# A hyperedge product of a four-layer graph network as two float32r passes, with its low part made on VectorE

## What is computed

```python
H = (adj != 0).astype(x.dtype)           # [N,C,C] indicator
w = adj.reshape(N, -1)[:, :C]            # first row of adj
Dn = jnp.einsum('nce,ne->nc', H, w)
Dn = jnp.where(Dn > 0, 1.0 / Dn, 0.0)
Be = H.sum(axis=1)
Be = jnp.where(Be > 0, 1.0 / Be, 0.0)
m = Be[:, :, None] * jnp.einsum('nce,nch->neh', H, xw)
out = Dn[:, :, None] * jnp.einsum('nce,neh->nch', H, m)
```

## Time and profile before

| | before |
|---|---|
| median of 3 runs | 1825.22 us (1825.14 to 1826.91) |
| the profiled execution: its time, its span | 1824.28 us, 1822.6 us |
| granted TensorE clock | 0.998 |
| busy: PE, DVE, ACT, POOL | 1771.0, 1416.4, 1443.2, 1442.6 us |
| one pass of the loop, from one e_cnt to that six passes on (767.32 to 1101.27 us) | 55.66 us |

### The profile page before, as it was taken

The page is one execution under the profiler, slowest core; times in us unless marked ns, Lnnn a source line. Parts: engine busy times, 40 slices in busy tenths (PEclk is TensorE's granted clock), DMA queues, the critical chain, the costliest instruction groups (busy, mean ns, idle before and its releaser), DMA issues.

```text
span 1822.6 us, 52146 instructions
## 1 busy us (share of the span) xinstructions
PE 1771.0 (97%) x15358; PEld 1569.1 (86%) x15358; DVE 1416.4 (78%) x3910; ACT 1443.2 (79%) x4463; POOL 1442.6 (79%) x2857
## 2 busy tenths in 40 slices
PE   7999999999999999999999999999999999999997
PEld 6888888888888888888888888888888888888886
DVE  6878778777778787787777787877877777878776
ACT  4888778887788887788877888877888777888776
POOL 4787778887788877788877888777888778887776
PEclk9999999999999999999999999999999999999999
DMA  4011101111001111011110011110111100111000
GB/s 129 22 42 41 36 13 32 40 40 40 18 28 35 40 40 37 12 32 40 40 40 20 26 35 40 40 37 12 32 40 40 40 20 26 35 40 40 29 9 22
DMA packets 93590, 62.94 MB, mean 35 GB/s; under 512 B 8430, under 2 KB 92924, under 8 KB 93564
## 3 DMA queue, kind: packets, MB, share of 16 engines
q1 hardware_dynamic: 92748, 61.58, 11.3%
q10 hardware_dynamic: 816, 1.05, 0.2%
HBM read 45.82 MB, written 16.78 MB: 34 GB/s over the span
## 4 chain that ended last, share of the span: by engine, by line
PE 62%; POOL 13%; issue 9%; DVE 8%; ACT 5%; ACTq 1%; SPq 1%; DMA 0%; POOLq 0%; DVEq 0%
PE ps L512 32%; PE ps L585 6%; PE ps L593 4%; PE ps L606 3%; POOL hT L928 3%; PE ps L617 3%; PE ps L528 3%; PE ps L576 3%; POOL ln_rs L882 3%; PE ps L496 3%; DVE z L1111 2%; ACT z L781 2%; PE ps L523 2%; POOL c L966 2%; POOL hb L934 2%
## 5 line engine op out<-in xcount | busy, mean ns | idle before, releaser
L781 ACT ACTIVATE z<-z,z_max 128x128 f32<-128x128 f32 x1024 | 401.0, 403 | 53.2 <-DVE z_max L1122 50.0
L882 POOL TENSOR_TENSOR ln_rs<-ln_ve,minus_half 128x1 f32<-128x1 f32 x640 | 352.6, 551 | 50.2
L902 POOL TENSOR_TENSOR z<-z,z_rcp 128x1024 f32<-128x1024 f32 x128 | 242.9, 1897 | 26.6 <-DVE z_rcp L1129 26.6
L885 POOL TENSOR_SCALAR ln_nm<-ln_mv,ln_rs 128x1 f32<-128x1 f32 x640 | 169.3, 264 | 109.8 <-POOL ln_rs L882 109.8
L880 POOL TENSOR_TENSOR ln_ve<-ln_mv,eps_col 128x1 f32<-128x1 f32 x640 | 121.8, 190 | 160.0 <-DVE ln_mv L1035 157.7
L1111 DVE SCALAR_TENSOR_TENSOR z<-ps,a_hold 128x512 f32<-128x512 f32 x256 | 171.1, 679 | 52.0 <-PE ps L576 48.7
L512 PE MATMUL ps<-w2T,mnT 128*128 128x256 f32 x1536 | 208.1, 287 | 0.0
L512 PE MATMUL ps<-w1T,txT 128*128 128x512 f32 x768 | 203.4, 400 | 0.9 <-DVE txT L1045 0.9
L781 ACT ACTIVATION_READ_ACCUMULATOR z<-z,z_max 128x1 f32 x1024 | 204.4, 200 | 0.0
L512 PEld LDWEIGHTS ps<-w2T,mnT 128*128 128x128 f32 x1536 | 188.8, 188 | 5.6 <-DVE mnT L1045 0.2
L1122 DVE TENSOR_REDUCE z_max<-z 128x4 f32<-128x512 f32 x256 | 169.5, 673 | 0.1
(11 more groups left out here) (154 smaller groups left out, 4864.4 us busy)
## 6 DMA issues: line engine op xcount, KB each, us to landing
x_in<-in_x_dram SPq DMA_DIRECT2D x128, 128.0 KB, 2.2
a_hold<-in_adj_dram SPq DMA_DIRECT2D x128, 128.0 KB, 2.2
out_dram<-y_out SPq DMA_DIRECT2D x128, 128.0 KB, 1.7
a_in<-in_adj_dram SPq DMA_DIRECT2D x128, 64.0 KB, 1.9
h<-in_L_gnn_W_dram SPq DMA_DIRECT2D x2, 512.0 KB, 5.7
x<-in_L_gnn_Wqk_dram ACTq DMA_DIRECT2D x1, 512.0 KB, 4.0
y_out<-in_L_gnn_W_dram ACTq DMA_DIRECT2D x1, 256.0 KB, 4.6
y_out<-in_L_gnn_Wv_dram ACTq DMA_DIRECT2D x1, 256.0 KB, 4.9
```

The source lines that it names most:

```text
L781: m = act.activation(z[:, g % 2, h, :], z[:, g % 2, h, :], ACT.Exp, bias=z_max[:, g % 2, h:h + 1], accum_out=z_sum[:, g % 2, h:h + 1])
L882: pool.tensor_tensor(rs[n][:, g:g + 1], ve[n][:, g:g + 1], minus_half[:, :], ALU.pow).then_inc(root_made[n], 1)
L885: pool.tensor_scalar(nm[n][:, g:g + 1], mv[n][:, g, 0:1], rs[n][:, g:g + 1], -1.0, ALU.mult, ALU.mult).then_inc(shift_made[n], 1)
L902: pool.tensor_tensor(zg, zg, z_rcp[:, g % 2, :].unsqueeze(2).to_broadcast([P, HEADS, P]), ALU.mult)\
```

## The change

The product `mp` becomes two float32r passes that accumulate in PSUM. The indicator hT is exactly 0 or 1 and is now stored as float32r; hb gets a high and a low part. POOL makes the high part from a rounded reciprocal `r_hi`. A new DVE step `hbl` stands right behind `ecnt` in both order texts and makes three things: the low part of the weight column, `r_lo` = e_rcp - r_hi, and the low part of hb, hT times r_lo. DVE's `ecnt` also makes r_hi. PE waits for `hb_made` before the high pass and for `hb_lo_made` before the low one. The other order texts are as they were.

```diff
-        ln4_aggr.1 ecnt.0+ mn_lo.2 z1.0+ mn_lo.3 zmax1.0+ y.2 z0.0+ ln4_stats.2 zmax0.0+ ln4_aggr.2 y.3
+        ln4_aggr.1 ecnt.0+ hbl.0+ mn_lo.2 z1.0+ mn_lo.3 zmax1.0+ y.2 z0.0+ ln4_stats.2 zmax0.0+ ln4_aggr.2 y.3
...
-        hT, hb, mp = sb("hT", G, P + 1), sb("hb", G, P + 2), sb("mp", G, P + 2)
+        hT = ctx.enter_context(nc.sbuf_tensor("hT", [P, G, P + 1], F32R))
+        hb, mp = parts("hb", G, P + 2), sb("mp", G, P + 2)
+        r_hi, r_lo = ctx.enter_context(nc.sbuf_tensor("r_hi", [P, G], F32R)), sb("r_lo", G)
...
             def mp_(a, g, o):
-                room(1, not need(hb_made, a))
-                return pe.matmul(o[:, 0:P + 2], hT[:, g, 0:P], hb[:, g, :], start=True, stop=True)
+                need(hb_made, a)
+                for part in (HI, LO):
+                    room(2 - part)
+                    if part == LO:
+                        need(hb_lo_made, a)
+                    m = pe.matmul(o[:, 0:P + 2], hT[:, g, 0:P], hb[:, part, g, :], start=(part == HI), stop=(part == LO))
+                return m
...
             def hb_(q, g):
                 pool.wait_ge(hT_made, q + 1)
-                pool.wait_ge(ercp_made, q + 1)
+                pool.wait_ge(rhi_made, q + 1)
                 after(pool, made["mp"], q * G)
-                pool.tensor_tensor(hb[:, :, 0:P], hT[:, :, 0:P], e_rcp[:, :].unsqueeze(2).to_broadcast([P, G, P]), ALU.mult)\
+                pool.tensor_tensor(hb[:, HI, :, 0:P], hT[:, :, 0:P].bitcast(F32),
+                                   r_hi[:, :].bitcast(F32).unsqueeze(2).to_broadcast([P, G, P]), ALU.mult)\
                     .then_inc(hb_made, 1)
...
-                dve.tensor_reduce(e_cnt[:, :], hT[:, :, :], AX.X, ALU.add).then_inc(cnt_made, 1)
-                dve.wait_ge(cnt_made, q + 1)
-                dve.reciprocal(e_rcp[:, :], e_cnt[:, :]).then_inc(ercp_made, 1)
+                dve.tensor_reduce(e_cnt[:, :], hT[:, :, :].bitcast(F32), AX.X, ALU.add).then_inc(edge_step, 1)
+                dve.wait_ge(edge_step, q * 4 + 1)
+                dve.reciprocal(e_rcp[:, :], e_cnt[:, :]).then_inc(edge_step, 1)
+                dve.wait_ge(edge_step, q * 4 + 2)
+                dve.tensor_copy(r_hi[:, :], e_rcp[:, :]).then_inc(rhi_made, 1)
+
+            def hbl(q, g, o):
+                after(dve, made["mp"], q * G)
+                dve.wait_ge(col_made, q + 1)
+                dve.tensor_tensor(hb[:, LO, :, P:P + 1], aT[:, :, 0:1], hb[:, HI, :, P:P + 1].bitcast(F32), ALU.subtract)\
+                    .then_inc(edge_step, 1)
+                dve.wait_ge(rhi_made, q + 1)
+                dve.tensor_tensor(r_lo[:, :], e_rcp[:, :], r_hi[:, :].bitcast(F32), ALU.subtract).then_inc(edge_step, 1)
+                dve.wait_ge(edge_step, q * 4 + 4)
+                dve.tensor_tensor(hb[:, LO, :, 0:P], hT[:, :, 0:P].bitcast(F32),
+                                  r_lo[:, :].unsqueeze(2).to_broadcast([P, G, P]), ALU.mult).then_inc(hb_lo_made, 1)
```

More of the change, by code:

```diff
@@ L110 @@
         turnlo.11+ ln1_stats.2+ ln1_aggr.2+ v1.3+ ln1_stats.3+ ln1_aggr.3+ x2t_lo.0+ turnlo.12+ turnlo.13+
-        turnlo.14+ x2t_lo.1+ x2t_lo.2+ x2t_lo.3+ turnlo.15+ turnlo.16+ c2lo.0+ lo_wo.0+ turnlo.17+ ecnt.0+
+        turnlo.14+ x2t_lo.1+ x2t_lo.2+ x2t_lo.3+ turnlo.15+ turnlo.16+ c2lo.0+ lo_wo.0+ turnlo.17+ ecnt.0+ hbl.0+
         turnlo.18+ turnlo.19+ scale.0+ scale.1+ z1.0+ zmax1.0+ z0.0+ scale.2+ zmax0.0+ scale.3+ z0.1+ z1.1+
@@ L156 @@
 HI, LO = 0, 1
-PASSES = {"at": 1, "ax": 2, "x1t": 2, "amx": 1, "wt": 1, "pb": 1, "x2t": 2, "mp": 1, "sc0": 4, "sc1": 4, "pt": 8, "cx": 8,
+PASSES = {"at": 1, "ax": 2, "x1t": 2, "amx": 1, "wt": 1, "pb": 1, "x2t": 2, "mp": 2, "sc0": 4, "sc1": 4, "pt": 8, "cx": 8,
           "tx": 2, "mn": 4, "y": 12, "turn": 1, "gram": 1, "c2": 1, "bw": 1}
@@ L285, in build @@
             "xb_made", "wm_made", "p_bias_made", "p_exp_made", "p_rcp_made"))
-        hT_made, col_made, cnt_made, ercp_made, hb_made = (sem(n) for n in (
-            "hT_made", "col_made", "cnt_made", "ercp_made", "hb_made"))
+        hT_made, col_made, edge_step, rhi_made, hb_made, hb_lo_made = (sem(n) for n in (
+            "hT_made", "col_made", "edge_step", "rhi_made", "hb_made", "hb_lo_made"))
         dsum_made, dmax_made, dpos_made, drcp_made, dhalf_made, dinv_made, dcnt_made, c3_half, c3_made = (sem(n) for n in (
@@ L659, in weights @@
                     need(read["turn"], a, last_turn["w1"])
-            counted_by_group = {read[s].name for s in per_group} | {s.name for s in (amT_made, wm_made, hb_made, col_made)}
+            counted_by_group = {read[s].name for s in per_group} | {s.name for s in (amT_made, wm_made, hb_made, hb_lo_made, col_made)}
             stages = {"at": at, "ax": ax, "h0": h0, "x1t": x1t, "amx": amx_, "xg": xg, "wt": wt, "pb": pb, "v1": v1,
@@ L754, in aT_free @@
                 after(act, amT_made, q)
-                after(act, hT_made, q)
-                after(act, col_made, q)
+                after(act, hb_lo_made, q)
             def mp_free(q, g):
@@ L775, in hbc @@
                 after(act, made["mp"], q * G)
-                act.copy(hb[:, :, P:P + 1], aT[:, :, 0:1]).then_inc(col_made, 1)
+                act.copy(hb[:, HI, :, P:P + 1], aT[:, :, 0:1]).then_inc(col_made, 1)
             def attn(q, g, half):
@@ L926, in hT_ @@
                 after(pool, made["mp"], q * G)
-                after(pool, cnt_made, q)
+                after(pool, edge_step, q * 4)
                 pool.tensor_scalar(hT[:, :, 0:P], aT[:, :, :], 0.0, 0.0, ALU.is_equal, ALU.is_equal).then_inc(hT_made, 1)
@@ L1183, in split @@
                 return run
-            stages = {"asum": asum, "h0": h0, "xg": xg, "wmax": wmax, "wnorm": wnorm, "pcol": pcol, "v1": v1, "ecnt": ecnt,
+            stages = {"asum": asum, "h0": h0, "xg": xg, "wmax": wmax, "wnorm": wnorm, "pcol": pcol, "v1": v1, "ecnt": ecnt, "hbl": hbl,
                       "drcp": drcp, "z0": z_(0), "z1": z_(1), "zmax0": zmax(0), "zmax1": zmax(1), "wo": wo, "h1": h1_, "y": y,
@@ L1217, in _ @@
             dve.memset(eps4_col[:, :], EPS / 4)
-            dve.memset(hT[:, :, P:P + 1], TINY)
+            dve.memset(hT[:, :, P:P + 1].bitcast(F32), TINY)
             dve.memset(p_row[:, :], 0.0)
-            dve.memset(hb[:, :, P + 1:P + 2], 1.0)
+            dve.memset(hb[:, HI, :, P + 1:P + 2].bitcast(F32), 1.0)
+            dve.memset(hb[:, LO, :, P + 1:P + 2].bitcast(F32), 0.0)
             walk(FIRST, -1)
```

## The result

| | before | after |
|---|---|---|
| median | 1825.14 us (1823.25 to 1826.91, 5 runs) | 1834.51 us (1833.5 to 1838.71, 5 runs) |
| profiled execution, span | 1822.6 us | 1832.7 us |
| one loop pass, e_cnt to e_cnt | 55.66 us | 55.98 us (771.20 to 827.18) |
| ratio after/before | | 1.0057, 95% interval 1.0042 to 1.0071 |

The change makes the kernel 9.4 us slower. The forecast was 1835.9 us, and the loop pass grew by 0.32 us where 0.33 was forecast. Part of that closeness is luck: two errors on the way, each as large as the forecast itself, cancel. ScalarE's exp0.0 came 0.32 us later than forecast, and 0.33 us were given back where the forecast had nothing.

A forecast was written before the change was run, and what follows sets the result against it. PE, 97% busy, was taken as nearly the bound, with a chain through other engines in each pass. 31 x 0.33 = 10.2 us plus 0.5 gave 10.7, from 1824.28 to 1835.0, median 1835.9 us; 8-in-10 range 1828 to 1858.

The forecast's parts named there:

- Where the delay starts: On PE, y.2 starts 0.06 us after DVE's mn_lo.2 ends, so TensorE was said to have no slack there.
- DVE's delay of 0.97 us: Four DVE instructions behind the reciprocal, the product priced 0.69 us, move mn_lo.2 0.97 us later, bounds 0.6 and 1.2.
- POOL's part is free: r_hi is ready 0.2 us after the reciprocal's end at 656.90; POOL takes up hb only at 657.85.
- What PE gives back: Lost PE time absorbs delay: 0.19 us in y.2 and y.3, 0.32 at the third mp product, 0.39 before v2.1.
- The narrow pass: A float32r pass of 130 columns takes 0.11 us, decided by weight loads, so 0.22 per product, as long as before.
- cheap rival: A narrow pass takes only 0.062 us; exp1.0 and three copies then set exp0.0, +0.24 per pass, 1833.1 us; chance 0.13.
- dear case: A narrow pass takes 0.22 us, 0.44 per product; exp0.0 comes 1.00 later per pass, 1856.7 us; chance 0.20.
- ACT decides, +0.33 per pass: The third mp product's copy makes ACT's exp0.0 0.33 us late; the dense work behind it gives nothing back.
- taken up elsewhere: Small DVE steps cost half and ACT's stretch to v2.2 hides a gap: under 0.1 us left, 1828 us; chance 0.07.
- The first filling: The pipeline's first filling has one more such delay, between 0 and 0.97 us, taken as 0.5 us.
- Faster: TensorE's own work decides, y.2 doesn't wait for mn_lo.2, each of 128 products saves 0.10 us: 1812.4 us; chance 0.05.

The follow-up runs named there:

- e2: Changed kernel with hb's low part zero from the start, step hbl gone, both float32r passes kept, four waits per aT copy as before: 1826.93 us, ratio 1.0013 to before.
- e4: Changed kernel with hT made by DVE ahead of e_cnt instead of by POOL: 1804.27 us, ratio 0.9891 to the kernel before.
- e1: Changed kernel with all DVE steps kept but the product one plain f32 product again: 1837.43 us, ratio 1.0070 to the kernel before.
- e8: Changed kernel with each float32r pass of the product streaming 240 instead of 130 columns: 1834.54 us, ratio 1.0034 to the kernel before.
- e9: Changed kernel whose low pass loads 64 of 128 stationary columns and doesn't add to the high pass: 1835.99 us, ratio 1.0060 to the kernel before.
- e3: Changed kernel with only the high float32r pass, step hbl gone, four waits per aT copy as before: 1827.52 us, ratio 1.0014 to the kernel before.
- e11: Kernel before with the waits hT_made and col_made ahead of each aT copy replaced by one, hb_made: 1820.18 us, ratio 0.9976 to before.
- e12: Kernel before with hT on DVE and the two waits ahead of each aT copy replaced by one: 1798.77 us, ratio 0.9856 to before.
- e5: Kernel before with hT made by DVE ahead of e_cnt, still four waits ahead of each aT copy: 1806.38 us, ratio 0.9881 to before.
- e10: Changed kernel with the waits hT_made and col_made put back ahead of each aT copy on ACT: 1846.8 us, ratio 1.0119 to the kernel before.
- e7: Changed kernel with step hbl moved behind zmax1.0 instead of ahead of mn_lo.2: 1881.13 us, ratio 1.0278 to the kernel before.

## Why the prediction was right, and where it was not

**Where the delay starts.** Right. The prediction saw that y.2 starts 0.06 us after mn_lo.2 ends and called it slackless; after the change PE waits there 31 times, and the waits vanish with the steps (e2) or when they move into DVE's idle time (e4). e1 and e2 show that in the place where the steps stand nothing else of the change costs.

**DVE's delay of 0.97 us.** Wrong, 1.42. The small steps were sized right (0.16 to 0.17 against 0.18, gaps included). The failed step is the price of the 128x512 product, "priced as its neighbours, 0.69 us". Its neighbours read PSUM or have one operand; it reads two from SBUF beside POOL's x2c.0 and had to wait for it. 1.14 against 0.69 is the whole error. The prediction's statement that POOL's part is free was wrong for the same reason: hb lasts 1.48 us. This harmed little: the two x3b run from 775.24 for 1.44 us, so x3b.2 ends at 775.96, and DVE reads y.2 at 776.07, as zmax1.0 ends.

**What PE gives back.** The places were right, the sizes too large. Of the 0.19 us in y.2 and y.3 only 0.09 was given back, of the 0.39 before v2.1 0.26; the 0.32 at the third product was taken up whole, with 0.05 more. 1.40 at y.2 is 0.68 at v2.1, 0.72 less, where the prediction had 0.90 to give.

**The narrow pass.** Right: 0.11 us apart but for the first, 0.10 on average, set by the load (e8, e9). Its price came from the difference of two load records, 0.82 ns per column, and not from the length of one, 188 ns for 128 columns; the 64-column loads of e9 (137 ns) lie on the same line. The cheap rival would have put six passes into 0.37 us, the dear one into 1.3; it was 0.62. But e3 shows that this term hardly mattered: even a pass that vanishes leaves the time where it is. The prediction gave the dear case 0.20 of its chance, on this term. A dear pass was not built, so whether it would have cost its 31 us is open.

**ACT decides, +0.33 per pass.** The place was right and both its parts wrong. exp0.0 came 0.65 late, not 0.33: with mn_lo.2 at +1.42, zmax1.0 and so exp1.0 were late by 1.09 (776.11, 4.91 after e_cnt, against 3.82), and exp1.0 with the three mp copies set exp0.0, not the third product. That is the shape the prediction had given to its cheap rival. Then ACT gave back 0.33 where "ACT works almost without a rest" allowed nothing. This is the second failed step: the prediction put nothing for the semaphore wait that the change itself takes away. 0.18 of the 0.33 is this spare wait ahead of each copy, as e11 shows on the kernel before (the copy of v2.2 at 10.48 instead of 10.66); the pitch of a group of four copies, 1.09 us for records of 0.26, was in the trace to be read. The other 0.15 lies ahead of the first copy. y_out.3 follows v2.1's copy after 0.32 us before and 0.25 after (1054.33 to 1054.65, 1060.47 to 1060.72), since it had to wait for POOL's root before; the remaining 0.08 stays open. So the rival "taken up elsewhere" held in part, together with a delay twice as large. Without that wait in the kernel before the same change would have cost some 15 us instead of 9.4, so the forecast of 10.7 us hit the number by this as well.

**The first filling.** The 0.5 us for it was not needed: from the first e_cnt to the last the kernels take 1726.4 and 1736.9 us, 10.5 more, and the whole span grew by 10.1.

**Faster.** It would have needed slack at y.2, and PE's work to decide. Neither holds where hT stands on POOL: e3 took 128 passes away and gained nothing.

## What to carry to other kernels

Before putting work on an engine, find where in a pass it idles and what it idles for. Here four steps cost some 15 us on one side of DVE's longest wait (after against e11) and nothing that was traced to them on the other (e4 against e12), and taking over the very step that it waited for brought the kernel to 20 us below before. Compare kernels that differ in one thing: the pair e4 and e5 looked equal only because a spare wait on one side hid what the change costs on the other. A DVE instruction with two SBUF operands must be priced together with what GpSimd does at that moment. On an engine that is dense and on the path, count its semaphore waits too, those long met included, and merge those that imply each other.

## What the runs showed of the hardware that was not expected

- A semaphore wait that is already met cost ScalarE some 0.04 us at the head of an instruction: four copies of 128x128 take 0.95, 1.09 and 1.19 us with three, four and five waits each, while each record stays 0.26 us, and the copy behind them comes 0.18 us earlier with four waits less (e11) and 0.30 us later with eight more (e10).
- That DVE and GpSimd wait for each other also hits tiny instructions: a 128x4 subtraction of 0.16 us took 0.77 beside POOL's x3b, and a 128x1 step of POOL's took 0.54 instead of 0.19.
- An f32 product of 128x130 and a pair of float32r passes of that size take nearly the same time in a row. Six records take 0.67 us in e1 and 0.62 in the kernel after, by their chain rows.
- Float32r passes of 512 columns over x2T start 0.227 us apart in the kernels made from before and 0.232 in those made from after, though nothing of these passes was edited. The cause is open.
- In e7, whose PE stands idle 0.81 us per pass for the low part, the granted clock fell to half for 3.4 us in 20 passes of the loop, and each of them took 1.2 us longer than the others.
